# A six-layer attention kernel on one core: places of side work inside a slot moved, and one write moved ahead of the row loads

## The reference, cut to what matters

```python
for i in range(NL):                      # NL = 6, D = 256, H = 16 heads of 16, DFF = 1024
    xn = _adaln(x, noise_emb, n1_w[i], n1_b[i])
    q, k, v = split(xn @ qkv_w[i].T)     # q and k are rotated (rope)
    x = x + _attn(q, k, v, src_mask) @ so_w[i].T
    xn = _adaln(x, noise_emb, n2_w[i], n2_b[i])
    # cross attention: q from xn, k and v from the context (512 tokens)
    x = x + _attn(q, k, v, ctx_mask) @ co_w[i].T
    xn = _adaln(x, noise_emb, n3_w[i], n3_b[i])
    h = gelu(xn @ f1_w[i].T + f1_b[i])
    x = x + (h @ f2_w[i].T + f2_b[i])
# then: x = x + experts(_layernorm(x)), top 2 of 8 experts, capacity 640 each
```

## Time and profile before

| | |
|---|---|
| median of 3 runs | 4339.0 us (4333.73 to 4340.74) |
| the profiled execution, its own time | 4337.09 us |
| its span, first to last instruction | 4335.3 us |
| slots 0 to 48, from the first pass-1 matmul to the end of pass 2 | 81.6 to 3986.1 us |
| experts and the end | 3986.1 to 4335.3 us |
| PE busy | 3833.6 us (88%) |
| DVE, ACT, POOL busy | 2841.1 (66%), 2498.6 (58%), 1148.4 us (26%) |
| mean granted TensorE clock | 0.966 |

### The profile page before, as it was taken

The page is one execution under the profiler, slowest core; times in us unless marked ns, Lnnn a source line. Parts: engine busy times, 40 slices in busy tenths (PEclk is TensorE's granted clock), DMA queues, the critical chain, the costliest instruction groups (busy, mean ns, idle before and its releaser), DMA issues. The chain is left out here.

```text
span 4335.3 us, 66534 instructions
## 1 busy us (share of the span) xinstructions
PE 3833.6 (88%) x19478; PEld 1695.2 (39%) x19478; DVE 2841.1 (66%) x4476; ACT 2498.6 (58%) x4206; POOL 1148.4 (26%) x1280
## 2 busy tenths in 40 slices
PE   3899899899899899899999899999999999897558
PEld 1233344433344433344433344433344433343446
DVE  6788766688666688766688766588766688751411
ACT  1577655577655567655567655567655577654112
POOL 3233222232222232322232322232322232301043
PEclk8999999999999999999999999999999999999779
DMA  5655534445533355433356443456443366521235
GB/s 160 157 153 145 131 80 94 107 137 145 131 81 91 97 145 141 132 90 82 93 150 148 125 95 82 94 145 153 123 99 80 91 171 154 132 54 46 68 103 112
DMA packets 334220, 500.30 MB, mean 115 GB/s; under 512 B 53705, under 2 KB 242257, under 8 KB 333521
## 3 DMA queue, kind: packets, MB, share of 16 engines
q1 hardware_dynamic: 289680, 430.95, 39.0%
q0 software_dynamic: 44160, 64.73, 6.3%
HBM read 278.54 MB, written 222.58 MB: 116 GB/s over the span
## 5 line engine op out<-in xcount | busy, mean ns | idle before, releaser
L908 ACT ACTIVATE prob<-ps 128x512 f32<-128x512 f32 x3072 | 1751.3, 595 | 1249.8 <-PE ps L832 1246.9
L1070 DVE TENSOR_REDUCE negmax<-ps 128x2 f32<-128x1024 f32 x1536 | 1814.8, 1217 | 362.4 <-PE ps L859 332.5
L832 PE MATMUL ps<-qstack,kstack 114*128 114x512 bf16 x3072 | 1144.6, 390 | 118.0 <-ACT prob L908 99.0
L845 PE MATMUL psv<-prob,v 128*32 128x512 f32 x6144 | 826.7, 610 | 0.0
L832 PEld LDWEIGHTS ps<-qstack,kstack 114*128 114x128 bf16 x3072 | 273.9, 97 | 1269.3 <-ACT prob L908 935.7
L859 PE MATMUL ps<-kstack,qstack 49*128 49x512 bf16 x3072 | 487.8, 387 | 78.7 <-DVE negmax L1070 53.3
L677 POOL TENSOR_TENSOR pool_fence<-eps 128x1 f32<-128x1 f32 x288 | 55.2, 192 | 1688.0 <-ACT mrow L975 1026.5
L807 PE MATMUL side<-nT,wf 128*128 128x256 f32 x1536 | 375.0, 387 | 31.9 <-ACT mrow L975 18.3
L1106 DVE TENSOR_SCALAR hT<-side,f1b 128x256 f32<-128x256 f32 x384 | 167.5, 478 | 295.6 <-PE side L807 295.5
L818 PE MATMUL side<-wf,hT 128*128 128x256 f32 x1536 | 350.1, 381 | 3.5 <-DVE x L1113 1.8
L807 PEld LDWEIGHTS side<-nT,wf 128*128 128x128 f32 x1536 | 285.4, 191 | 88.2 <-ACT mrow L975 22.3
(11 more groups left out here) (170 smaller groups left out, 3626.8 us busy)
## 6 DMA issues: line engine op xcount, KB each, us to landing
bounce<-parts SPq DMA_DIRECT2D x480, 256.0 KB, 2.5
qstack<-bounce SPq DMA_DIRECT2D x384, 192.0 KB, 6.1
kstack<-bounce SPq DMA_DIRECT2D x384, 192.0 KB, 6.6
value_sums<-osum SPq DMA_DIRECT2D x192, 256.0 KB, 6.5
bounce<-low SPq DMA_DIRECT2D x96, 256.0 KB, 2.1
hT<-value_sums POOLq DMA_DIRECT2D x96, 256.0 KB, 4.8
nT<-inverse POOLq DMA_DIRECT2D x96, 256.0 KB, 3.8
ctxT<-in_ctxT SPq DMA_DIRECT2D x24, 512.0 KB, 5.3
```

Of the source, the lines that this page charges most:

```text
L832: nc.tensor.matmul(ps2[:, n % RING2, :], kk[0:ROWS, h, kt * P:(kt + 1) * P], q[0:ROWS, h, :], start=True, stop=True).then_inc(s_p2full, 1)
L845: mm = nc.tensor.matmul(psv[32 * i:32 * i + 32, 0, :], v[j % 2][:, kt, (HD + 1) * h:(HD + 1) * h + 32], prob[:, 4 * (u % 2) + i, :], start ...
L908: nc.scalar.activation(prob[:, 4 * (u % 2) + i, :], ps2[:, n % RING2, :], ACT.Exp, scale=HD ** -0.5).then_inc(s_prob, 1)
L1070: nc.vector.tensor_reduce(out_at, ps1[:, 2 * (n % 2):2 * (n % 2) + 2, :], AX, ALU.max, negate=True).then_inc(s_p1free, 1)
```

## The change

1. SP: `load_first(k + 1, 1)` and `load_second(k + 1, 1)` stood at the end of slot k, ahead of `write_sums(k - 1, 3)` at the start of slot k + 1. Now they stand in slot k + 1 behind that write. In slot 1 they now also stand behind the loads of norm weights.
2. Short slots: HT 6, 8 becomes 6, 7; HQ 9, 11 becomes 8, 9; SPLIT 14, 16, 19, 21 becomes 12, 14, 18, 20; RECIP 8 becomes 6; NORM 14, 15 becomes 10, 11.
3. Long slots: HT 6, 8 becomes 6, 7; HQ 14, 15 becomes 8, 9 (now ahead of O, which keeps 11, 12); HK 16, 18 becomes 13, 15; LT 17, 19 becomes 16, 17; F1 20 to 27 becomes 18 to 25; F2 28 to 31 becomes 26, 28, 30, 31; SPLIT, GELU, PARTS and NORM move with them.

```diff
 SHORT = {
-    "M": [25, 0], "HV": [1, 3], "HT": [6, 8], "HQ": [9, 11], "HK": [12, 14], "O": [18, 20],
-    "SPLIT": (14, 16, 19, 21), "PARTS": 23, "RECIP": 8, "NORM": (14, 15),
+    "M": [25, 0], "HV": [1, 3], "HT": [6, 7], "HQ": [8, 9], "HK": [12, 14], "O": [18, 20],
+    "SPLIT": (12, 14, 18, 20), "PARTS": 23, "RECIP": 6, "NORM": (10, 11),
...
 LONG = {
-    "M": [27, 0], "HV": [1, 3], "HT": [6, 8], "O": [11, 12], "HQ": [14, 15], "HK": [16, 18], "LT": [17, 19],
-    "F1": [20, 21, 22, 23, 24, 25, 26, 27], "F2": [28, 29, 30, 31],
-    "SPLIT": (17, 19, 21, 23), "GELU": (24, 28), "PARTS": 25, "RECIP": 5, "NORM": (9, 10),
+    "M": [27, 0], "HV": [1, 3], "HT": [6, 7], "HQ": [8, 9], "O": [11, 12], "HK": [13, 15], "LT": [16, 17],
+    "F1": [18, 19, 20, 21, 22, 23, 24, 25], "F2": [26, 28, 30, 31],
+    "SPLIT": (13, 15, 18, 20), "GELU": (22, 26), "PARTS": 24, "RECIP": 5, "NORM": (8, 9),
...
-    "LN_LT": dict(stats=[12, 12, 12, 12], aggregate=13, guess=13, newton=14, tiles=[14, 14, 15, 15]),
+    "LN_LT": dict(stats=[12, 12, 12, 12], aggregate=13, guess=14, newton=14, tiles=[14, 14, 15, 15]),
...
                 if tail:
                     write_sums(k - 2, 3)
+                if k and p1:
+                    load_first(k, 1)
+                    load_second(k, 1)
                 if k % NJ == 2 and p1:
...
                     write_sums(k - 1, 1)
                     write_sums(k - 1, 2)
-                if head:
-                    load_first(k + 1, 1)
-                    load_second(k + 1, 1)
```

## The result

| | before | after |
|---|---|---|
| median | 4339.87 us (4 runs, 4333.73 to 4342.37) | 4436.13 us (4 runs, 4430.65 to 4451.81) |
| ratio, 95% interval | | 1.023 (1.0201 to 1.0259) |
| profiled execution, own time | 4337.09 us | 4451.81 us |
| span | 4335.3 us | 4450.1 us |
| mean granted TensorE clock | 0.966 | 0.944 |

The forecast was 4270 us, 1.6% faster, in a range of 4228 to 4330. The measurement is 166 us above it and outside the range.

A forecast was written before the change was run, and what follows sets the result against it. PE's order was taken to set the time, its waits being what can be won; -35 (later long), -26 (first long), -7 (short) and -1 made -69, less 2 for slot 1, -67: 4270 us, range 4228 to 4330.

The forecast's parts named there:

- Part 1: SP's write ahead of the row loads: denominators' 6.8 us wait goes in first long slots, factors come 1 us later.
- Part 4: 24 short slots: smaller waits against a 1.6 us wait in unit 6, net about -0.3 us each, -7 us.
- Part 2: 15 later long slots: no wait before O, longer one before LT, -2.3 us each, -35 us.
- The clock term: Later long slots: O's pause goes, LT's grows, so as many slots at low clock (8 of 15): 0 us.
- moves whole: First long slots, bound of -1 us: the wait moves whole from the denominators to the factors.
- Part 3: Six first long slots: denominators' wait and its low clock go, -4.3 us each, -26 us, bounds -7 and -1 each.
- Part 5: The rest: DVE's stall after the jump back 0, bounds -8 and +4; slots 47 and 48 gain 1 us.
- A: Rival: row loads delay POOL's loads by the full 2.8 us, O waits in all long slots; 4299 us, chance 0.15.
- B: Rival: longer pauses before LT and in unit 6 drop the clock, +50 us; 4320 us, chance 0.14.
- C: Rival: short slots' multiplication and LT's tile get no turn between POOL's rope steps; +45, 4382 us, chance 0.07.
- D: Rival: DVE keeps up, LT's pause stays 1.6 us, clock never drops; -130, 4207 us, chance 0.12.
- three signs of failure: Unit 6 wait of 2.8 us or more, mean clock below 0.95, or any PE wait for row loads.

The follow-up runs named there:

- E4: The change with the ten row loads moved back behind the write of the first group of value sums: 4289.03 us, ratio 0.9885.
- E2: The change's tables of places with the SP order of the kernel before: 4323.58 us, ratio 0.9959.
- E6: E5 with short slots' multiplications at places 11 and 12 and all four norm tiles before LT at place 14: 4184.99 us, ratio 0.9639.
- E5: E4 with the loads of cross and self weights also moved behind the row loads: 4240.16 us, ratio 0.977.
- E1: The kernel before with only the change's SP order, row loads behind the write of the fourth group: 4409.42 us, ratio 1.0161.
- E9: E5 with only the short slots' multiplications moved to places 11 and 12: 4222.3 us, ratio 0.9728.
- E3: The change with the short slots' two multiplications back at places 14 and 15: 4383.02 us, ratio 1.0102.

## Why the prediction was wrong

**The step that failed** is in Part 1: the row loads "start at 5 us and compete with POOL's four loads of the tail", for which I took 1 us, with bounds 0 and 2.8 us. Three things in it were wrong.

- **The size.** The bound came from one row, the denominators' load beside context and weight loads. Beside the rows it added 3.1 us (2.1 to 5.2), to the write of the reciprocals 3.7 (2.4 to 6.1) and to the load of the sums 4.9 (4.8 to 9.7).
- **The time.** I had the rows over by 17 us, from ten loads and a write that took 14 us in slot 14. I did not add that the sums' two loads of 256 KB run in the same stretch: the rows landed at 20.1 us.
- **The link.** Nothing stood in the sum for the reciprocals' write, issued at 14.4 us, the one link of the chain between DVE's fixed place for the reciprocal and the factors. The denominators, which I did price, landed at 12.4 us, still ahead of DVE's reciprocal at 13.3.

In slot 15 the factors came at 27.7 us and not at 22.5: 6.2 us later than before, 4.1 of them by the write and 2.1 on the way back, where the sum had 1. O was to be free for work at 25.6, and DVE is done 2.6 us behind the factors: 4.7 us late by that working, and 4.4 were measured.

**Part 4, short slots.** The sum counted DVE's and PE's order and took the factors as given. In slot 11 they landed at 27.1 us, and DVE was ready for them at 25.6 (971.28 less the 1.51 us wait and the slot's start). Two other terms held: 1.35 us in E4 for 1.6, and the 1.04 us wait for the exponential in unit 11 is gone. This omission was the dearest, with +89 for -7. The part has a slip as well: -0.55 and +0.4 make -0.15 us a slot and not -0.3, which moves the forecast by under 4 us.

**Parts 2 and 3.** LT, F1 and M came as costed. Where the factors are in time, the sum of Part 2 comes out: later long slots fell by 2.4 us on the mean in E4 and 2.1 in E2 where -2.3 was forecast, and the two of E4 in which the clock stayed up took 94.0 and 93.7 us (94 forecast). The clock term did not hold: "I keep the same count: 0". In E4, where O does not wait in them, the clock is low in 13 of the 15 (3.4 us of it, on the mean), where before it was low in 7 (the prediction counts 8). The pause before LT, now 2.2 us, is the only one of over 0.9 us in these slots, and in 11 of the 13 the granted clock falls within 1.2 us of its end. The denominators' wait of first long slots is gone, as forecast, and its 6.8 us came back as a wait for factors: 3.9 us before O in slot 14 and the low clock. That is the bound "moves whole" of Part 3, and past it: +0.4 us a slot, where the bound was -1.

**Part 5** allowed -8 to +4 for slots that begin a pass. DVE's stall there did shrink, by 2.7 us, but the cross weights, now issued behind the rows, met the chain: the load of the factors took 8.1 us in slot 10, and PE lost 7.4 us in unit 6.

**The rivals.** A was the mechanism, with a chance of 0.15 and a price of 29 us; B was right that the low clock would be nearly everywhere, 0.14 and 50 us, though by the factors' waits: with the pause in unit 6 at the forecast 1.35 us it came in 2 of 18 short slots (E4), with 2.5 to 4.5 us in 14 of 18 (the change). Both were there at once, and A's price had the same bound of 2.8 us for one load. C, the one rival that was slower, is refuted in its reason: in E4 the first multiplication ends 1.1 us before POOL's second rope step. The Trainium skill's rule ("SBUF — State Buffer", "SBUF: two separate sides") that the loser of the shared port pair blocks for the whole instruction agrees with the 1.02 us that the multiplication took beside L649 where it takes 0.67 alone; it does not follow from it that a queued POOL step goes first. D wanted LT's pause at 1.6 us and the clock up, and neither came; E6, where that pause is 0.5 us and rows and weights are late too, reached 4185 us. Of my three signs of failure two came, a wait in unit 6 of 2.8 us or more and a mean clock below 0.95 (0.944). The third, "any wait of PE for row loads", did not: the rows themselves were never late, only what flew beside them.

For a loader's order the Trainium skill has a rule that I had not weighed ("DMA: Bandwidth & Descriptors", "Issuing engines are not separate DMA queues"): transfers started by SP and by POOL end up on the same 16 DMA engines and interleave. The landings above agree with it: POOL's write took 5.8 us with SP's row loads in flight and 1.8 without.

## What to carry to other kernels

When loads are moved, draw the stretch from their issue to their last landing, and look at every small transfer of another engine's chain that falls into it, at its writes too; the one to price is the one that starts behind a fixed point and has no slack behind it. In this kernel bulk loads whose users come late (here 30 us and more) were best put behind such a chain, though that is later than they could go: 104 to 147 us of 4340. Two edits can cost more together than one by one: here +69 and -17 us made +96, since one made the data later and the other its use earlier.

## What the runs showed of the hardware

- A DMA of 32 KB was not cheap in proportion beside the row loads: 1.8 to 2.1 us without them (E4, E5), 5 to 6 us with them (the change, E1). The row for slot 15 has 84 GB/s on the mean; the row loads are in flight for 15 us of its 102.
- With data in flight, DVE stands longer behind the loop's jump back. The timeline of DVE at the start of slot 10, after:

```profile
874.40 1.23 DVE L1071 TENSOR_REDUCE negmax<-ps 128x2 f32<-128x1024 f32 x1 [2.84 <-issue]
```

  Before it was 5.54 us, with the row loads in flight at the border; in E1, which only moves them away, 3.11. Over the four passes it was 5.5 to 6.2 us before and 2.8 to 3.1 in E1. No releaser is shown in either. That it is the loading of instructions is only argued, from packets of the two instruction queues that fall into this stretch.
- In later long slots with one pause of PE of 2.2 us the clock was low in 13 (E4) and 14 (E9) of 15; with waits of 1.3 and 0.5 us in its place in 5 of 15 (E6).
- DVE's multiplication has no fixed price beside POOL: 0.67 us alone, 1.02 when it met the last 0.5 us of a rope step (E4), 3.15 for two that met L658 and a rope step back to back (E3). It got its turn between two POOL steps each time, and ended 0.55 us behind the one that it met.

Left open: whether the write of 32 KB waits in its own queue or on the DMA engines; these rows don't tell the two apart, and it wasn't tried to put it on SP's queue. Nor was it tried to take the reciprocal of long slots earlier.
